# One spreading matmul for the masked rows' weights, and x's transposes earlier in their slots, in a fused attention and output kernel

## The reference

```python
x = x + layernorm(attn(layernorm(x)))
x = x + layernorm(ffn(layernorm(x)))

# attn, per batch row and head
qkv    = x @ w_qkv.T + b_qkv
scores = einsum('bhfc,bhtc->bhft', k, q)
scores = where(triu(ones(s, s)), scores, -10000.0)
attn   = softmax(scores, axis=-2)
vals   = einsum('bhft,bhfc->bhtc', attn, v)
out    = vals @ w_o.T + b_o

# ffn: hidden @ W.T + b, and a low-rank term of one of four ranks, chosen by a gate
```

## Time and profile before

| what | value |
|---|---|
| median of three runs | 1555.43 us (1554.69 to 1556.09) |
| the profiled execution | 1554.09 us, of it the span on the core 1552.3 us |
| PE busy | 1494.7 us, 96% of the span |
| DVE, ACT, POOL busy | 971.5, 702.4 and 571.7 us |
| mean granted TensorE clock | 0.987 of full speed |

### The profile page before, as it was taken

One profiled execution on the slowest core, in us unless ns is written; L12 is line 12 of the kernel. 1 busy time (PEld: TensorE's weight loads), 2 busy tenths in 40 slices (PEclk: granted clock), 3 DMA queues, 4 the chain that ended last, 5 costly groups with the idle time before them and its releaser, 6 DMA issues. The chain is left out here.

```text
span 1552.3 us, 25053 instructions
## 1 busy us (share of the span) xinstructions
PE 1494.7 (96%) x8160; PEld 1320.2 (85%) x8160; DVE 971.5 (63%) x2105; ACT 702.4 (45%) x1499; POOL 571.7 (37%) x1098
## 2 busy tenths in 40 slices
PE   7999999999999999999999679999999999999996
PEld 5888888888888888888888569999999999999996
DVE  7475575664765755756646656666666666666663
ACT  5364564573664645645635533333333333333331
POOL 2251351442342513514412534444443443334433
PEclk9999999999999999999999889999999999999998
DMA  6212112121112131121201712222222221111111
GB/s 240 72 42 84 42 31 88 34 54 61 44 48 71 39 88 37 37 82 34 54 21 38 237 59 68 69 68 68 68 68 68 68 68 63 59 61 59 62 61 41
DMA packets 46926, 102.92 MB, mean 66 GB/s; under 512 B 5040, under 2 KB 21424, under 8 KB 46896
## 3 DMA queue, kind: packets, MB, share of 16 engines
q1 hardware_dynamic: 46896, 102.54, 21.2%
HBM read 60.06 MB, written 25.69 MB: 55 GB/s over the span
## 5 line engine op out<-in xcount | busy, mean ns | idle before, releaser
L1471 PE MATMUL ps_f<-wagh,x2Th 128*128 128x364 f32 x768 | 256.5, 334 | 4.4 <-DVE f L1333 2.9
L1471 PE MATMUL ps_f<-wagl,x2Th 128*128 128x364 f32 x768 | 253.7, 330 | 0.0
L1471 PE MATMUL ps_f<-wagh,x2Tl 128*128 128x364 f32 x768 | 253.2, 330 | 0.0
L914 PE MATMUL ps_o<-xTh,wh 128*128 128x512 f32 x504 | 210.2, 417 | 9.1 <-DVE xTl L541 5.3
L914 PE MATMUL ps_o<-xTh,wl 128*128 128x512 f32 x504 | 198.6, 394 | 0.0
L914 PE MATMUL ps_o<-xTl,wh 128*128 128x512 f32 x504 | 197.2, 391 | 0.0
L1471 PEld LDWEIGHTS ps_f<-wagh,x2Th 128*128 128x128 f32 x768 | 145.5, 189 | 7.2 <-issue 5.0
L1471 PEld LDWEIGHTS ps_f<-wagl,x2Th 128*128 128x128 f32 x768 | 145.7, 190 | 1.3
L1471 PEld LDWEIGHTS ps_f<-wagh,x2Tl 128*128 128x128 f32 x768 | 145.5, 189 | 0.0
L445 POOL TENSOR_SCALAR pr<-pr,rden 128x128 f32<-128x128 f32 (+3 forms) x256 | 136.5, 552 | 0.0
L758 ACT ACTIVATE pr<-ps_s,nm 128x128 f32<-128x128 f32 (+3 forms) x256 | 130.4, 521 | 0.1
(11 more groups left out here) (171 smaller groups left out, 3532.1 us busy)
## 6 DMA issues: line engine op xcount, KB each, us to landing
kst<-kst SPq DMA_DIRECT2D x64, 256.0 KB, 3.6
xt<-in_x SPq DMA_DIRECT2D x32, 512.0 KB, 4.0
out<-outs SPq DMA_DIRECT2D x32, 512.0 KB, 3.1
xs<-in_x SPq DMA_DIRECT2D x24, 512.0 KB, 4.3
valsT<-vt SPq DMA_DIRECT2D x64, 128.0 KB, 2.3
vraw<-valsT SPq DMA_DIRECT2D x32, 256.0 KB, 4.2
raw<-in_wqkvT SPq DMA_DIRECT2D x12, 512.0 KB, 6.1
wag_raw<-in_wagT SPq DMA_DIRECT2D x8, 546.0 KB, 5.2
```

The source lines that it names most:

```text
L914: done = pe.matmul(ps[:, :], w[:, k, c:c + P], xT[:, k, :], start=(k == 0 and w is wh and xT is xTh), stop=(k == KD - 1 and w is wl), skip ...
L1471: last = pe.matmul(ps_f[:, g, 0:GW], a[:, k, :], w[:, k, cols], start=(k == 0 and a is x2Th and w is wagh), stop=False, skip_group_check=True)
```

## The change

Per head PE did three matmuls of 128 columns, each with a weight of its own (a column of `wn` repeated) against the identity. Now POOL first writes a diagonal matrix of `wn` for each of three key tiles into `WT` (128x384), and PE does one matmul of 384 columns with a weight of ones; ACT's copy of the result goes back into the same `WT`. POOL's instruction stands between `wn` and the scaling of `pr`, and waits until the values of two heads before have read that `WT`. The spread also moves on PE: it stood behind the first six matmuls of the slot's first step, and stands behind the whole step (12 matmuls, in slot 1 24). The constant `identr` goes, `ones` comes.

The pairs of x at place 1 go ahead of the transposes of the weights, and those at place 2 ahead of `steps(h, 1)`. ACT's `x_back` moves likewise: place 1 ahead of `p_hi`, place 2 ahead of the late exponentials of slot 4 and of the projection's high parts. On DVE, `x_low(1)` of slot 5 goes ahead of `vals_sum` and `p_lo`.

```diff
@@ normalise, POOL
                 pool.tensor_tensor(wn[:, q, :], wm[:, q, :], rden[:, q, :], ALU.mult).then_inc(wn_done, 1)
+                pool.wait_ge(wn_done, H + 1)
+                if h > 1:
+
+                    pool.wait_ge(pv_done, H - 1)
+                pool.tensor_tensor(WT[:, q, :].rearrange("p (i t) -> p i t", i=3),
+                                   ident[:, :].unsqueeze(1).to_broadcast([P, 3, P]),
+                                   wn[:, q, 0:3].unsqueeze(2).to_broadcast([P, 3, P]), ALU.mult).then_inc(d_ready, 1)
                 for i in range(NT):
@@ body, DVE
                     if h in SOON:
                         lows(h, 0, b, last)
+                    if h == X_SLOT and not last:
+                        x_low(1, b + 1)
...
                             p_lo(h - 1, g, b)
-                    if h == X_SLOT and not last:
-                        x_low(1, b + 1)
@@ body, ACT
+                    if h != 3:
+                        backs(h, 1, b, last)
                     if 1 <= h <= NH:
                         for g in range(2):
                             p_hi(h - 1, g, b)
-                    if h != 3:
-                        backs(h, 1, b, last)
+                    backs(h, 2, b, last)
                     if h < NH and late:
                         exps(h, b)
                     if h not in SOON:
                         highs(h, 0, b, last)
-                    backs(h, 2, b, last)
@@ masked_weights, PE
-                pe.wait_ge(wn_done, H + 1)
+                pe.wait_ge(d_ready, H + 1)
                 if h > 0:
                     pe.wait_ge(t_lo, 3 * H - 1)
-                for i in range(3):
-                    last = pe.matmul(ps_t[1][:, i * P:(i + 1) * P], wn[:, h % 2, i:i + 1].to_broadcast([P, P]),
-                                     identr[:, :], start=True, stop=True)
-                last.then_inc(t_full[1], 1)
+                pe.matmul(ps_t[1][:, 0:3 * P], ones[:, 0:1].to_broadcast([P, P]), WT[:, h % 2, :],
+                          start=True, stop=True).then_inc(t_full[1], 1)
@@ steps, PE
+                    step(kind, p, row, ks, last)
                     if n == 0 and part == 0 and 1 <= h <= NH:
 
-                        step(kind, p, row, ks[:2], last)
                         masked_weights(h - 1, b)
-                        step(kind, p, row, ks[2:], last)
-                    else:
-                        step(kind, p, row, ks, last)
@@ body, PE
                         values(h - 2, b)
+                    turns(h, 1, b, last)
                     if 1 <= h <= NH:
                         transpose_p(h - 1, 0, b)
                         transpose_p(h - 1, 1, b)
-                    turns(h, 1, b, last)
+                    turns(h, 2, b, last)
                     steps(h, 1, b, last)
-                    turns(h, 2, b, last)
```

More of the change, by code:

```diff
@@ L163, in attention_phase @@
         WT = sb("WT", [P, 2, 3 * P], F32R)
-        identr = sb("identr", [P, P], F32R)
+        ones = sb("ones", [P, 2], F32R)
         pr = sb("pr", [P, 2, PT_N], F32)
@@ L187, in attention_phase @@
         rden = sb("rden", [P, 2, 4], F32)
-        wn = sb("wn", [P, 2, 4], F32R)
+        wn = sb("wn", [P, 2, 4], F32)
         ps_s = ctx.enter_context(nc.psum_tensor("ps_s", [P, 3 * 512], F32))
@@ L239, in attention_phase @@
         wn_done = sem("wn_done")
+        d_ready = sem("d_ready")
         p_ready = sem("p_ready")
@@ L480, in _ @@
             pool.memset(wm[:, :, :], 0.0).then_inc(consts, 1)
+            pool.memset(ones[:, :].bitcast(F32), 1.0).then_inc(consts, 1)
             pool.memset(hold[:, 1:2], 0.0).then_inc(vals_ready, 1)
@@ L485, in _ @@
             pool.memset(hold[:, 0:1], 0.0).then_inc(held, 1)
-            pool.wait_ge(consts, 11)
+            pool.wait_ge(consts, 12)
             pool.affine_select(out=ident[:, :], in_=ident[:, :], compare_op=ALU.not_equal, fill=1.0, base=0,
@@ L491, in _ @@
                                pattern=[[-1, P]], channel_multiplier=1).then_inc(consts, 1)
-            pool.wait_ge(consts, 13)
-            pool.tensor_scalar(identr[:, :], ident[:, :], 1.0, 1.0, ALU.mult, ALU.mult).then_inc(consts, 1)
             for t in range(NT):
```

## The result

The changed kernel takes 1582.03 us (median of 4 runs, 1581.39 to 1582.58) against 1555.76 for the kernel before beside it (1554.69 to 1556.39): a ratio of 1.0169, 95% interval 1.0152 to 1.0187. It is slower by 26 us. The forecast said slower by some 18. The time lies inside the wide range of 1561 to 1584, near its upper end, and 3 us outside the forecast's own range of 1563 to 1579.

The account below looks back on a forecast made before the run. PE was taken to bound the kernel, busy for all but one of a block's 106.60 us. Terms of +1.95 per block gave +13.7 over seven, plus last block +1.5 and clock +3: +18.2, so 1573 us; range 1561 to 1584, own 1563 to 1579.

Parts of the forecast that it names:

- the main term: Slot 3: x tile 2's transposes, moved ahead of twelve matmuls, wait for POOL's normalised tile; +2.35 us per block.
- rival C: Whole kernel: slower by far, clock falling in every block and last block at its upper bound; +28, 1583 us; 15%.
- Pair (3, 0): Slot 4: PE's moved transposes wait for normalised x tile 3; +0.75 us per block, bounds 0.35 and 1.15.
- slot 1: With no values to cover the later spread, PE waits for ACT's copy of it; +0.36 us per block.
- the scores of head 5: Slot 4: they wait for head 4's exponentials, now behind a late copy of x on ACT; +0.3 us per block.
- The two old waits: Slots 4 and 6: PE's waits for ACT's copy and DVE's low part of x go; -0.45 and -0.98 per block.
- The clock: Loop: the granted clock falls after the new 2.35 us wait; two falls of 1.5, +3 us, ends none and seven.
- The last block: Slots 6 to 8: POOL's diagonal lies on the path for heads 6 and 7; +1.5 us, bounds 0.5 and 4.
- The larger wait for `pr`: Last block: PE's wait for POOL before the transposes, 2.51 us before the change, was to grow.
- The later spread: Slots 2 to 8: ACT's copy is covered by values or projection between spread and transposes, so no wait comes.
- Slot 5: ACT's copy delays x's split, or `x_low(1)` delays p_lo; slot 6's wait returns at about 0.9 per block, bounds 0 and 1.3.

Follow-up runs that it names:

- e9: The changed kernel with DVE's statistics of x tile 2 moved into slot 2 and those of tile 3 ahead in slot 3: 1566.11 us.
- e8: The changed kernel with POOL's diagonal instruction done twice per head, the second writing the same values: 1590.00 us.
- e2: The kernel before with only the moves of x (transposes, copies, `x_low(1)`), the spread old and in its old place: 1581.68 us.
- e1: The changed kernel with all moves of x's work undone, keeping the diagonal, the single spreading matmul and its later place: 1556.91 us.
- e6: e1 with the spread after nine matmuls of its step instead of all twelve: 1553.61 us.
- e3: The changed kernel with x's transposes of place 2 and their copies put back behind the second step: 1565.88 us.

## Why the prediction was right, and where it was mis-sized

**The range.** The direction and the main term held, but not the size. The time lies in the wide range because rival C, at 1583, had been taken into it. What C supposed did not come: the clock fell in two blocks and not in all seven, and the last block grew by 1.3 and not by 4. So the measured time agrees with C's by luck, and the forecast's own sum was some 8 us short.

**The main term.** Pair (2, 0): 2.35 forecast, 2.35 measured, by the chain that the prediction followed: PE's half of k, DVE, the row maxima of head 3, the statistics, POOL. e9 shows the link that matters: with only the statistics moved, the wait for POOL goes. e8 shows that POOL's new work has no part in it.

**Pair (3, 0), slot 1, the scores of head 5:** 0.75, 0.36 and 0.3 forecast; 0.63, 0.31 and 0.28 measured. The two old waits went, as counted.

**The clock:** two falls, 3 us in all, as priced. Two was a guess between none and seven, so that the number fits is luck. A fall came within 2 us after the wait for tile 2 in the third and the sixth block, and not in the five others, which have the same wait. What decides between them isn't shown.

**The last block:** +1.5 forecast, +1.3 measured. That the 1.3 is the diagonal's isn't shown: e2 has no diagonal, its last block runs the instructions of before, and it takes 104.44, 1.05 longer than before, at a mean granted clock of 0.90 there (0.93 before, 0.92 in the changed kernel). The diagonal took 0.83, not 1.0, in all 64 cases. The larger wait for `pr` did not come (1.9 in all, against 2.5 before); PE waits for the diagonal itself, ahead of head 7's spread:

```profile
905.35 0.69 PE L971 MATMUL ps_t<-WT,ones 128*128 128x384 f32 x1 [2.67 <-POOL WT L448]
```

The prediction weighed the Trainium skill there (SBUF — State Buffer, "Who interferes with whom"), by which the diagonal of head 7 would stand behind DVE's subtractions. It does not: it starts at 904.46, ahead of DVE's subtraction at 904.59, and it takes 0.83 as elsewhere.

**The sum was too small, 1.95 per block instead of 3.40, and in two terms.**

*The later spread.* The prediction said that in slots 2 to 8 the copy is covered by the work between, and booked -1.28 + 0.36 = -0.92 for the spread and its place. e1 measures this part alone at +0.06. The saving is real (about 1.2), but in slot 5 ACT has, behind the spread, the copy, the exponentials and P's high half in one chain, and 0.40 goes to P's last transposes. In slot 7 0.31 goes the same way, there by DVE's row maxima. The step that failed, "so it is covered", asked only whether PE waits for the copy, and not who stands behind the copy on ACT; the prediction asked that for slot 5 alone, and looked for the price at slot 6. e6 shows that with the spread 0.7 us earlier the waits of slots 1 and 5 are gone, while slot 7's stays.

*Slot 5.* The prediction put 0.9 for what would take the place of the wait at slot 6, with bounds 0 and 1.3, and named DVE's p_lo behind `x_low(1)` as a candidate. That is where it came, 1.83 in the changed kernel. The moves alone (e2) make 1.45 of it: `x_low(1)` takes 1.74 us instead of 0.68, since at the new place POOL is subtracting, too. The Trainium skill (the same section) has it that a DVE instruction with two SBUF inputs and a GpSimd one that reads SBUF contend, and that the second to come stands still. The trace agrees twice: DVE's row ends 0.55 after POOL's, and POOL's next subtraction takes 1.72 instead of 1.29. I had applied that rule to the last block and not to the move on DVE, where it counted. The trace of the kernel before had the price, for the one of `x_low`'s subtractions that ran beside POOL's there (count, busy us, mean ns):

```profile
L541 DVE TENSOR_TENSOR xTl<-x,xTh 128x512 fp32r<-128x512 f32 x7 | 12.5, 1779 | 0.0
```

The other 0.4 is the spread's.

Together: the spread +0.06 instead of -0.92, the moves +3.17 (e2) instead of +2.87, and 0.17 that only both make. (The prediction's 0.9 for slot 5 stood for ACT's copy and for `x_low(1)` together; here it is counted with the moves.) Smaller terms that the sum did not have, 0.24 in slot 4 and 0.44 in slot 7, are among these.

## What to carry to other kernels

When work is moved up on the engine that bounds, follow back the chain of its input, past the engine named as the releaser: POOL was named here, and DVE's order was the cause, as e9 shows. An instruction put later on the bounding engine costs even where its own consumer is covered, if its consumer's engine has more in line behind it; look for the place between too early and too late, as e6 does. When an instruction with two inputs from SBUF is moved on DVE, see what POOL reads at that time.

## What the hardware showed that I had not expected

A DVE subtraction of 128x512 got next to nothing done beside POOL's: 1.74 and 1.25 us instead of 0.68, each ending 0.55 us after POOL's own end. The granted clock fell to 0.50, the 1.2 GHz level, for 2.8 us or more after a wait of 2.2 in two blocks of seven, while in e9, whose longest wait is 1.7, it stayed at 1.00 through the loop; e3, whose longest wait is 1.7 as well, had three falls. So the length of the longest wait alone does not decide it.
